# Low parts of three weight tiles by accumulating transfers, the graph layer's degrees moved to batch 1's step, and four loads behind a copy, in a fused two-layer graph kernel

## What is computed

```python
def layer0(x, mask):                        # per batch
    xc = x.T
    h = relu(bn1(conv1d(xc, conv1_w)))      # 1 tap
    h = bn2(conv1d(h, conv2_w, pad=8))      # 17 taps
    x_conv = relu(h + xc).T
    s = x @ w_se.T + b_se                   # 3 values per node
    dist = sq[:, None] + sq[None, :] - 2 * s @ s.T
    A = exp(-dist) * mask
    x_nmp = A @ relu(x @ w_msg.T + b_msg)
    gi = concat(x_conv, x_nmp) @ w_ih.T + b_ih
    gh = x @ w_hh.T + b_hh                  # three gates: r, z, n
    r, z = sigmoid(gi_r + gh_r), sigmoid(gi_z + gh_z)
    return (1 - z) * tanh(gi_n + r * gh_n) + z * x
x = layernorm(x + layer0(x, adj))
# layer 1: the first 25 nodes alone, five groups of nodes; per group
#   A = adj_g + I;  deg = A.sum(-1);  N = deg**-.5 * A * deg**-.5
#   h = relu(N @ (x_g @ W1) + b1);  out = relu(N @ (h @ W2) + b2)
#   fused[nodes of g] += softmax(fusion_w)[g] * out
x = layernorm(x + layer1(x, adj))
```

## Time and profile before

| | us |
|---|---|
| median of three runs | 357.65 |
| lowest and highest of them | 357.35, 362.7 |
| the profiled execution's own time | 358.44 |
| its span, from the first to the last instruction | 356.6 |
| TensorE busy in it | 339.5 (95%) |
| VectorE busy | 319.4 (90%) |
| ScalarE busy | 236.8 (66%) |
| GpSimd busy | 94.2 (26%) |

### The profile page before, as it was taken

How to read it: one execution, slowest core, us unless ns; L and a number is a source line. 1 busy time by engine, 2 the same in 40 slices (tenths; PEclk the granted TensorE clock), 3 DMA queues, 4 the chain that set the end, 5 groups by cost and what they waited for, 6 DMA issues and landing times. The chain is left out here.

```text
span 356.6 us, 6244 instructions
## 1 busy us (share of the span) xinstructions
PE 339.5 (95%) x1767; PEld 275.7 (77%) x1767; DVE 319.4 (90%) x566; ACT 236.8 (66%) x410; POOL 94.2 (26%) x153
## 2 busy tenths in 40 slices
PE   4989999999999999999999999999999999999891
PEld 1577678986889688977988688968897798866670
DVE  2989999999999999999999899999999999896636
ACT  4383665748856696748764885669684886976752
POOL 4750001604050503222050505040231306052123
PEclk9989999999999999999999999999999999999997
DMA  6914241514043222604161403412260415301101
GB/s 195 307 26 130 83 132 44 170 31 148 18 129 129 74 76 61 211 0 147 36 202 34 147 13 103 156 55 92 55 193 25 147 31 147 119 22 36 29 2 53
DMA packets 30950, 33.95 MB, mean 95 GB/s; under 512 B 4884, under 2 KB 18124, under 8 KB 30932
## 3 DMA queue, kind: packets, MB, share of 16 engines
q1 hardware_dynamic: 30166, 33.55, 31.3%
q10 hardware_dynamic: 766, 0.18, 0.2%
HBM read 24.85 MB, written 4.40 MB: 82 GB/s over the span
## 5 line engine op out<-in xcount | busy, mean ns | idle before, releaser
L1276 POOL TENSOR_TENSOR base<-mv,vscale 128x4 f32<-128x4 f32 x16 | 6.0, 373 | 234.9 <-DVE mv L1405 228.2
L685 PE MATMUL p_outer<-t_h,w_h 128*128 128x344 f32 x131 | 41.9, 337 | 0.0
L685 PE MATMUL p_outer<-t_h,w_l 128*128 128x344 f32 x131 | 40.8, 328 | 0.0
L1373 DVE TENSOR_TENSOR am<-am,adj 128x512 f32<-128x512 f32 x64 | 40.0, 686 | 0.0
L1539 DVE TENSOR_TENSOR am_l<-am,am_h 128x2048 fp32r<-128x2048 f32 x15 | 34.3, 2287 | 1.8 <-ACT am_h L1130 1.8
L685 PE MATMUL p_middle<-t_h,w_h 128*128 128x344 f32 x90 | 28.6, 329 | 0.0
L1130 ACT ACTIVATE am_h<-am 128x2048 fp32r<-128x2048 f32 x15 | 28.5, 1901 | 0.0
L685 PE MATMUL p_middle<-t_h,w_l 128*128 128x344 f32 x90 | 28.0, 322 | 0.0
L685 PEld LDWEIGHTS p_outer<-t_h,w_h 128*128 128x128 f32 x131 | 25.0, 194 | 2.4 <-ACT t_h L1002 0.7
L1108 ACT ACTIVATE yoo<-yn,nb,rs 128x128 f32<-128x128 f32 x63 | 25.8, 483 | 0.0
L685 PEld LDWEIGHTS p_outer<-t_h,w_l 128*128 128x128 f32 x131 | 25.2, 195 | 0.3
(11 more groups left out here) (387 smaller groups left out, 1019.4 us busy)
## 6 DMA issues: line engine op xcount, KB each, us to landing
adj<-adjT SPq DMA_DIRECT2D x64, 256.0 KB, 3.2
xpad<-xT SPq DMA_DIRECT2D x17, 256.0 KB, 2.9
out<-yoo SPq DMA_DIRECT2D x16, 256.0 KB, 2.3
crossed<-left SPq DMA_DIRECT2D x31, 48.0 KB
left<-left SPq DMA_DIRECT2D x30, 48.0 KB
right<-left SPq DMA_DIRECT2D x30, 48.0 KB
wc<-w_c SPq DMA_DIRECT2D x2, 384.0 KB, 6.6
wraw<-g_w SPq DMA_DIRECT2D x1, 640.0 KB
```

The source lines that it names most:

```text
L685: return nc.tensor.matmul(out_, w, x, start=start, stop=stop, skip_group_check=True)
L1276: TT(base[:, 0:CH], mv[:, :, 1], vscale[:, 0:CH], ALU.mult)
L1373: TT(am[:, c, :], am[:, c, :], adj[:, c, :], ALU.mult).then_inc(s_am[c], 1)
```

## The change

1. `w0_l`, `w4_l` and `wg_l` are no longer subtracted on VectorE. ScalarE writes the high part, then the negated high part into the low tile, and GpSimd issues a DMA that adds the fp32 source to it (`accum_op=ALU.add`, from `wc2` and `wraw` in SBUF to the low tile in SBUF). On ScalarE the two tap groups move ahead of `w3_h`; GpSimd issues the three transfers after its last memset. TensorE waits for `s_wgacc` ahead of batch 0's gates and for `s_wacc` ahead of group 0 in the even steps. SP's load of `gw2` waits for `s_wgacc` too, and ScalarE waits for `s_wacc` ahead of `fe`, since `wc2` is overwritten later.
2. The loops' addition on `ac`, the eight degree products and the three degree instructions move from the first step to batch 1's: the addition behind `rows_val`, the products behind the transposes (into `p_outer`), the three instructions behind `inner`. Group 1 of that step waits for the degree copy, as it writes `p_outer`.
3. On SP the two loads of gate weights and the loads of batches 2 and 3 are issued after the first copy of `crossed`.

```diff
             load_adj(0, c)
-        sp.dma_start(wg[:, 0:2, :], w_ih[:, :, :]).then_inc(s_wgd, 16)
-        sp.dma_start(wg[:, 2, :], w_hh[:, :]).then_inc(s_wgd, 16)
-        sp.dma_start(xin[:, 2, :], xT[2, :, :]).then_inc(s_x[2], 16)
-        sp.dma_start(xin[:, 3, :], xT[3, :, :]).then_inc(s_x[3], 16)
-
         def spread_factors(q):
...
         sp.dma_start(full(crossed[0:KD, :]), full(left[32:32 + KD, :])).then_inc(s_right[0], 16)
+        sp.dma_start(wg[:, 0:2, :], w_ih[:, :, :]).then_inc(s_wgd, 16)
+        sp.dma_start(wg[:, 2, :], w_hh[:, :]).then_inc(s_wgd, 16)
+        sp.dma_start(xin[:, 2, :], xT[2, :, :]).then_inc(s_x[2], 16)
+        sp.dma_start(xin[:, 3, :], xT[3, :, :]).then_inc(s_x[3], 16)
         spread_factors(1)
...
         sp.dma_start(gb1[:], g_b1[:, :, :]).then_inc(s_gd, 16)
-        sp.wait_ge(s_wgs, 2)
+        sp.wait_ge(s_wgacc, 16)
         sp.dma_start(gw2, g_w2.rearrange("g (h p) o -> p g h o", p=128)).then_inc(s_gd, 16)
...
             for j in range(PAIRS):
-                last = mm(p_gi[0:CC, j:j + 1], ac[0:CC, j, :], cst[0:CC, C_ONE:C_ONE + 1])
+                last = mm(p_outer[0:CC, j:j + 1], ac[0:CC, j, :], cst[0:CC, C_ONE:C_ONE + 1])
             last.then_inc(s_deg, 1)
...
             last.then_inc(s_d, 1)
-            pe.wait_ge(s_t3h, 1); pe.wait_ge(s_whi, 1); pe.wait_ge(s_w0, 1)
+            pe.wait_ge(s_t3h, 1); pe.wait_ge(s_whi, 3); pe.wait_ge(s_w0, 1)
             stream(3, p_outer, s_t3l, 1, 1)
...
             msg(1, R_MSG)
-            pe.wait_ge(s_t12h, 1); pe.wait_ge(s_whi, 2); pe.wait_ge(s_w2, 1)
+            pe.wait_ge(s_t12h, 1); pe.wait_ge(s_whi, 4); pe.wait_ge(s_w2, 1)
             stream(1, p_middle, s_t12l, 1, 2)
-            pe.wait_ge(s_whi, 3); pe.wait_ge(s_v, 1)
+            pe.wait_ge(s_whi, 5); pe.wait_ge(s_v, 1)
             stream(2, p_outer, s_t12l, 1, 3)
...
             last.then_inc(s_nmp, 1)
-            pe.wait_ge(s_xh, 2); pe.wait_ge(s_xl, 2); pe.wait_ge(s_wgs, 2); pe.wait_ge(s_e[2], 1)
+            pe.wait_ge(s_xh, 2); pe.wait_ge(s_xl, 2); pe.wait_ge(s_wgs, 1); pe.wait_ge(s_wgacc, 16); pe.wait_ge(s_e[2], 1)
             gate(p_r, "r", 2, x_h[0][:], x_l[0][:], True, False)
...
             gate(p_gh, "n", 2, x_h[0][:], x_l[0][:], True, True).then_inc(s_gx, 1)
-            degrees()
             pe.wait_ge(s_nh, 1)
...
             gate(p_z, "z", 1, n_h[:], n_l[:], False, False)
-            pe.wait_ge(s_dg, 1)
             gate(p_gi, "n", 1, n_h[:], n_l[:], True, False)
...
             msg(q, R_MSG)
-            after(pe, s_t04h, n.pair(0)); after(pe, s_whi, 5); after(pe, s_wlo, 5)
+            after(pe, s_t04h, n.pair(0)); after(pe, s_wacc, 32)
             after(pe, s_pq, n.pair(1))
...
             turn(n)
+            if static(b, 1):
+                pe.wait_ge(s_h1, 4)
+                degrees()
...
                 after(pe, s_h1, n(3))
+                if static(b, 1):
+                    pe.wait_ge(s_dg, 1)
                 stream(1, p_outer, s_t12l, n.pair(1))
...
             A(m0, mt[:], ACT.Relu).then_inc(s_m0, 1)
+            for w_h, w_l, k in ((w0_h, w0_l, 0), (w4_h, w4_l, 2)):
+                act.wait_ge(s_w2d[k], 16)
+                A(w_h[:], wc2[:, k::3, :], ACT.Copy).then_inc(s_whi, 1)
+                act.wait_ge(s_whi, 1 + k // 2)
+                A(w_l[:], full(w_h[:]), ACT.Identity, scale=-1.0).then_inc(s_wneg, 1)
             act.wait_ge(s_wsum, 2)
...
             A(wg_h[:], wg, ACT.Copy).then_inc(s_wgs, 1)
+            act.wait_ge(s_wgs, 1)
+            A(wg_l[:], full(wg_h[:]), ACT.Identity, scale=-1.0).then_inc(s_wneg, 1)
             x_high(0, z, 2)
             x_high(0, z, 3)
-            A(w0_h[:], wc2[:, 0::3, :], ACT.Copy).then_inc(s_whi, 1)
             act.wait_ge(s_mt, 2)
...
             first_sum(o, p_middle, ev0)
-            A(w4_h[:], wc2[:, 2::3, :], ACT.Copy).then_inc(s_whi, 1)
             neighbours(z)
...
                 A(am[:, c, :], D_EVEN[c][:], ACT.Exp).then_inc(s_e[c], 1)
+            act.wait_ge(s_wacc, 32)
             act.wait_ge(s_fw, 2)
...
         nc.gpsimd.memset(x1[:], 0.0).then_inc(s_zero, 1)
+        pool.wait_ge(s_wneg, 1)
+        pool.dma_start(full(w0_l[:]), wc2[:, 0::3, :], accum_op=ALU.add).then_inc(s_wacc, 16)
+        pool.wait_ge(s_wneg, 2)
+        pool.dma_start(full(w4_l[:]), wc2[:, 2::3, :], accum_op=ALU.add).then_inc(s_wacc, 16)
+        pool.wait_ge(s_wneg, 3)
+        pool.dma_start(full(wg_l[:]), wg, accum_op=ALU.add).then_inc(s_wgacc, 16)
...
             msg_sum(z, 1, R_MSG)
-            dve.wait_ge(s_wgs, 1)
-            TT(wg_l[:], wg, full(wg_h[:]), ALU.subtract).then_inc(s_wgs, 1)
             msg_low(1, z, 1)
...
             TT(wc1_l[:], wc1[:], full(wc1_h[:]), ALU.subtract).then_inc(s_w1s, 1)
-            dve.wait_ge(s_whi, 4)
-            TT(w0_l[:], wc2[:, 0::3, :], full(w0_h[:]), ALU.subtract).then_inc(s_wlo, 1)
-            dve.wait_ge(s_acd, 32 * BLOCKS)
-            TT(ac[0:CC, :, :], ac[0:CC, :, :], cst[0:CC, C_ID:C_ID + CC].unsqueeze(1).broadcast_to([CC, PAIRS, CC]), ALU.add).then_inc(s_ac, 1)
             dve.wait_ge(s_sum[2], 1); dve.wait_ge(s_ev, 1)
...
             neighbours_low(z)
-            dve.wait_ge(s_whi, 5)
-            TT(w4_l[:], wc2[:, 2::3, :], full(w4_h[:]), ALU.subtract).then_inc(s_wlo, 1)
-            dve.wait_ge(s_deg, 1)
-            CP(dg[:, 0, :], p_gi[0:CC, 0:PAIRS]).then_inc(s_dg, 1)
             conv_low(z)
...
             x_low(0, z, 3)
-            dve.wait_ge(s_dg, 1)
-            TS(dg[:, 1, :], dg[:, 0, :], 0.0, None, ALU.is_equal).then_inc(s_dg, 1)
-            dve.wait_ge(s_dg, 2)
-            TT(dg[:, 2, :], dg[:, 0, :], dg[:, 1, :], ALU.add).then_inc(s_dg, 1)
             dve.wait_ge(s_gd, 48)
...
                 mask(z, 1, c)
+
+        def looped():
+
+            dve.wait_ge(s_acd, 32 * BLOCKS)
+            TT(ac[0:CC, :, :], ac[0:CC, :, :], cst[0:CC, C_ID:C_ID + CC].unsqueeze(1).broadcast_to([CC, PAIRS, CC]), ALU.add).then_inc(s_ac, 1)
+
+        def degrees():
+            dve.wait_ge(s_deg, 1)
+            CP(dg[:, 0, :], p_outer[0:CC, 0:PAIRS]).then_inc(s_dg, 1)
+            dve.wait_ge(s_dg, 1)
+            TS(dg[:, 1, :], dg[:, 0, :], 0.0, None, ALU.is_equal).then_inc(s_dg, 1)
+            dve.wait_ge(s_dg, 2)
+            TT(dg[:, 2, :], dg[:, 0, :], dg[:, 1, :], ALU.add).then_inc(s_dg, 1)
...
                 rows_val(n, 0)
+            if static(b, 1):
+                looped()
             if not more:
...
                 inner(n)
+                if static(b, 1):
+                    degrees()
                 rows_left(n, 0)
```

More of the change, by code:

```diff
@@ L203, in gnn_kernel @@
         s_prm = sem("s_prm"); s_shift = sem("s_shift"); s_f0 = sem("s_f0"); s_wsum = sem("s_wsum"); s_wtap = sem("s_wtap")
-        s_w1s = sem("s_w1s"); s_whi = sem("s_whi"); s_wlo = sem("s_wlo"); s_w4l = sem("s_w4l"); s_wgs = sem("s_wgs")
+        s_w1s = sem("s_w1s"); s_whi = sem("s_whi"); s_wlo = sem("s_wlo"); s_wneg = sem("s_wneg"); s_wacc = sem("s_wacc"); s_wgacc = sem("s_wgacc"); s_wgs = sem("s_wgs")
         s_ac = sem("s_ac")
@@ L1481, in first @@
                 neighbour_steps_first()
-                dve.wait_ge(s_whi, 1)
+                dve.wait_ge(s_whi, 3)
                 TT(w3_l[:], u3, full(w3_h[:]), ALU.subtract).then_inc(s_wlo, 1)
                 inner(o)
-                dve.wait_ge(s_whi, 2)
+                dve.wait_ge(s_whi, 4)
                 TT(w1_l[:], u1, full(w1_h[:]), ALU.subtract).then_inc(s_wlo, 1)
@@ L1489, in first @@
                 STT(tiles(cv, 2), both(p_middle, TILE3), prm[:, P_S2:P_S2 + 1], tiles(xpad[:, 0:2], 2), ALU.mult, ALU.add).then_inc(s_w2, 1)
-                dve.wait_ge(s_whi, 3)
+                dve.wait_ge(s_whi, 5)
                 TT(w2_l[:], u2, full(w2_h[:]), ALU.subtract).then_inc(s_wlo, 1)
```

## The result

| | before | after |
|---|---|---|
| median, us (runs) | 358.19 (4) | 365.22 (4), from 363.42 to 367.88 |
| ratio, 95% interval | 1 | 1.0195, from 1.0147 to 1.0244 |
| profiled execution; its span | 358.44; 356.6 | 367.88; 366.1 |
| the same kernel again, beside 29 runs of before | 358.06 | 367.12 (4), from 366.05 to 368.03; ratio 1.0239, from 1.0184 to 1.0294 |

The change costs 7 to 9 us, about 2%. I had forecast 357.3 and a range up to 361.5, so the time lies outside it. The two measurements, 7.0 and 9.1 over before, are of four runs each; the last experiment comes back to their difference. Some executions of a kernel take over 1.5% longer than its fastest, and a ratio leaves them out where a median does not, so the two can differ. The spread that I gave, 0.3%, is too small: the 29 executions of before take from 356.8 to 365.0 us.

The account below looks back on a forecast made before the run. Bound by when TensorE gets through the first step and when VectorE hands over after batch 1's. Terms + 1.2 + 0.2 + 0.3 − 0.2 − 0.7 − 0.5 = 0.3 us off the 357.65 median: 357.3, range 356.3 to 361.5.

Parts of the forecast that it names:

- step C: Loops' addition and degrees moved from the first step to batch 1's: 0.2 + 0.3 us gained, 0.7 + 0.5 lost.
- One wait may eat into this: First step: VectorE's maximum of fusion weights waits for all three graph loads; 0.2 us lost, at most 0.8, at least nothing.
- Step A: Crossed copy ahead of four loads closes TensorE's 1.30 us hole before the first distance product; 1.2 us gained.
- Step B: Low parts by accumulating transfers: VectorE freed, `wg_l` visible at 33.1, 0.35 us before batch 0's gates want it.
- the rival that I feared most: Late accumulation: batch 0's gates wait for `wg_l`; 2.8 us slower at a third rate, 6.3 at a quarter; chance 0.32.

Follow-up runs that it names:

- the last experiment: The changed kernel measured once more, unedited, beside the kernel before (e12_after_again): 367.12 us, ratio 1.0239.
- e5_deg_alone: The kernel before with only the loops' addition and the degrees moved to batch 1's step: 359.98 us, ratio 0.9998.
- e12_after_again: The changed kernel, unedited, measured again beside the kernel before: 367.12 us, ratio 1.0239.
- e3_no_acc: The changed kernel with the three low parts subtracted on VectorE again and no accumulating transfers: 360.9 us, ratio 1.0102.
- e10_wg_only: The changed kernel with only `wg_l` accumulated, the other low parts subtracted, and the fusion weights loaded first on their own semaphore: 358.97 us, ratio 1.0004.
- e6_crossed_alone: The kernel before with only the four loads moved behind the first crossed copy: 358.15 us, ratio 0.997.
- e1_fw_own: The changed kernel with the fusion weights' load ahead of the 28 small loads, on its own semaphore: 359.9 us, ratio 1.0061.
- e4_acc_alone: The kernel before with only the three accumulating transfers in place of the three subtractions: 360.97 us, ratio 1.0069.
- e8_fw_no_acc: The changed kernel with subtractions back and the fusion weights loaded first on their own semaphore: 358.58 us, ratio 0.9947.

## Why the prediction was wrong

**The step that failed** is the sentence in step C: "One wait may eat into this … I put 0.2 us here, at most 0.8." The mechanism was named, with its semaphore, its queue and the four issues in front; its size was wrong: 5.29 and 4.12 us, more than five times even its upper end. Three inputs were off. I counted 2 us of delay for `g_w2` and it was 7.66 and 5.96, mostly (4.14 and 3.70) because I let the 28 small loads be issued at their old rate beside 1.31 MB of accumulating traffic that I had myself put into the same stretch. I took the upper end from the quiet of 38 to 42 us, which is a row of a kernel without that traffic. And I took a little too little for the landing: 640 KB landed 5.7 and 6.1 us after its issue, where 40.1 − 34.85 = 5.25 was assumed. The upper end should have come from the nearest row of an issue beside full traffic.

**Step A** was right in its mechanism, and its size is open. The copy came sooner, and in no trace of the new order is there a hole. What that is worth depends on how large the hole would have been. From the start of `left` to batch 0's gates it takes 34.65 − 12.55 = 22.10 us in the profile of before, whose hole is 1.30 and whose clock then falls; 33.68 − 12.56 = 21.12 in e5_deg_alone, in the old order with a hole of 0.20 and no fall; and 33.95 − 12.84 = 21.11 in e12_after_again, in the new order. So the forecast 1.2 us are 1.0 against the one profile and nothing against the other. A fall of the clock at 20 to 26 us comes with the new order too (the first trace of after, e3_no_acc, e10_wg_only). Where nothing is won, TensorE waits for VectorE's `rz` and `w_l` instead, which the text had said "for a part". One profile's hole, the landing of one copy, was read as a property of the kernel. By time, e6_crossed_alone's interval of 0.9925 to 1.0014 allows anything from 2.7 us gained to 0.5 lost.

**Step B**'s wait was met, as forecast, and 1.3 us earlier than forecast (31.8 for 33.1). The sizes around it were off, and cancelled: issues of 1.68, 2.10 and 0.90 us where 1.0 was taken, but an earlier start (20.22 for 23.2), as GpSimd's `prm` instruction was shorter in that execution. So the rival that I feared most, `wg_l` late, is refuted for the changed kernel: the gates start 2.3 and 1.2 us after the landing in its two traces. It was near all the same: in e1_fw_own and e4_acc_alone the gates start right behind the landing, 0.43 us later than they could. The Trainium skill's formula (DMA: Bandwidth & Descriptors, Anatomy of one DMA — SWDGE (gpsimd) path) gives an estimate of 3.4 us for `wg_l`; the traces show 4.9 to 7.7 with adding (5.3 and 6.1 in the changed kernel) and 4.7 as a plain copy, so the measurement is above it in both. The damage of B went another way, through the DMA engines to SP's next issues, which the text didn't consider.

**Step C** in batch 1's step was put at 0.7 + 0.5 = 1.2 and measured 1.05 (e5_deg_alone 1.03, e8_fw_no_acc 1.06). The degree instructions behind `mt` cost the 0.5 forecast.

**VectorE's saved time**: `c_l` was expected near 37.9 and started at 38.50, 38.31 and 38.01. The text said that it follows `c_h`; it did not draw the conclusion that step B's 3 us of VectorE are then worth almost nothing at that point. They stand as 2.43 us of idle time ahead of `c_l`, and e10_wg_only shows the same with one subtraction.

**The lower clock** was missing from the sum as a consequence of a wait: 0.46 and 1.41 us behind the two waits. So was its fall in the tail, some 4 us in both profiled executions of the changed kernel; the profile of before doesn't have it. A range that reached only to the late `wg_l` left out that two waits can add to each other.

## What to carry to other kernels

When a change puts heavy traffic beside a list of small DMA issues, price the issues anew and follow the queue to its last member: here the first ten of 28 issues took about 1.03 us each where the first twelve had taken about 0.47, the rest stayed at 0.28, and what was late in the end was a load that nobody needed so early. Look for semaphores that count several loads of which the waiting instruction needs one; giving that one its own, and moving it ahead, took back 5.3 us. And before pricing a hole in one profile, ask whether it is a landing that another execution would show otherwise.
